# Cross attention of a gated decoder by whole sequences, with stacked hi/lo scores and a sum by a product, on one Trainium2 core

## The chip, the core and the metric

The kernel runs on one core of one Trainium2 chip. The metric is the device time of one execution in microseconds. The engines of a core are TensorE (PE; its weight loads are listed as PEld), VectorE (DVE), ScalarE (ACT), GpSimd (POOL) and SyncE (SP), each with its own queue of instructions, taken in the order in which they were written; they wait for one another through semaphores. SyncE's and ScalarE's queues also issue DMA transfers. Products go from SBUF to PSUM, which has 8 banks of 512 float32 columns.

## The reference

There are 16 sequences of 256 queries with 128 features, and 64 context rows for each. Cross attention has 16 heads of 8 features. What the change touches is this, once per layer:

```python
q, k, v = heads(norm(x) @ Wq.T [+ bq]), heads(ctx @ Wk.T [+ bk]), heads(ctx @ Wv.T [+ bv])
scores = einsum('bhqd,bhkd->bhqk', q, k) / sqrt(8)
scores = where(causal, scores, -inf)      # layer 0 only: key <= query
scores = where(mask, scores, -inf)        # layer 1: -1e10
out = softmax(scores) @ v
x = x + tanh(g) * (merge(out) @ Wo.T [+ bo])
```

Between the two cross attentions come two layers of local attention with an MLP, and at the end a mixture of experts; these are not changed.

## The kernel before

The program is a row of stages with all engines meeting between them: `Setup`, `Cross` for layer 0, `Local` and `Mlp` twice, `Cross` for layer 1, `Experts`. Setup loads the constants, computes keys (`kT`, features by keys) and values (`vall`) of all sequences and the rows of the masks.

`Cross` goes by tiles of 128 queries, 32 in all, two per sequence. `tensor`, `scalar`, `vector` and `gpsimd` each hold a loop over steps `s`, in which several tiles are at different points: in step `s` tile `s-2` is transposed, `s-3` becomes q, `s-4` gets its scores, `s-5` is transposed back, and so on up to `s-9`. The order within a step is written out by hand and is the order of that engine's queue. `after` waits for a count that frees a buffer.

For a tile, VectorE takes statistics (L225, L227), GpSimd the root (L232, L234), VectorE normalizes (L238), TensorE transposes (L412), ScalarE copies (L484), TensorE forms q (L419). ScalarE rounds q to the reduced-precision float32r as `qT` (L490), VectorE keeps the rest `qTr` (L550 in layer 0, L547 in layer 1). Keys are split in the same way into `kTh` (L513) and `kTr` (L515), and for each sequence GpSimd spreads both into block form, 128 features by 16 heads x 64 keys (L594). Scores are three products for each half of 512 columns (L438 to L440), a causal part from a 64-row identity (L442, only layer 0 and even tiles) and the pad row (L444, one row). VectorE takes the negated maxima (L564) and adds them (L567) into SBUF, ScalarE takes the exponential (L478). TensorE transposes that in eight parts (L458), ScalarE copies it (L503), and L468 multiplies it with `vpair`, in which each pair of heads has 32 columns: values, and two columns of ones, so that sums of the exponentials come out beside the values. ScalarE copies (L509), TensorE transposes (L425), VectorE takes the reciprocal of the sums (L529) and multiplies (L531), TensorE transposes once more (L451), ScalarE copies (L497), L403 is the output projection, L405 the bias of layer 1 from one row, and L520 updates x. In layer 0, the stage also normalizes the updated x into y (L225 to L238), which local attention reads.

SyncE issues only loads of later weights: 21 transfers in layer 0 (L185 to L205) and three of expert weights in layer 1 (L210 to L212).

## Time and profile before

| | us |
|---|---|
| three runs, median (lowest to highest) | 1428.67 (1428.21 to 1429.47) |
| profiled execution, its own time | 1427.41 |
| its span in the profile | 1425.6 |
| TensorE busy | 1276.2 (90%) |
| VectorE busy | 1107.3 (78%) |
| ScalarE busy | 832.5 (58%) |
| GpSimd busy | 866.1 (61%) |

A row of a view of busy times gives a stretch in us from the span's start, its length, then for PE, PEld, DVE, ACT and POOL the busy time and the number of instructions, then the granted clock of TensorE as a share of 2.4 GHz, the DMA engines' share and GB/s. A row of the timeline gives start, duration, engine, line, operation, output and inputs, shapes, how many were merged, and in brackets the idle time before it with what ended it. A row of a group gives line, engine, operation, names, shapes, count, then busy us and the mean in ns, then the idle time before it. Matmuls are pipelined: the distance of two starts is what one costs, its duration holds a latency. An f32 product that is not a transpose is two instructions.

### The profile page before, as it was taken

Reading aid. Unit: us, or ns where it says so; the run is one execution under the profiler, and the core shown is the slowest. Engines: PE = TensorE matmul, PEld = TensorE weight load, DVE = VectorE, ACT = ScalarE, POOL = GpSimd, SP = SyncE. Lnnn points to the kernel's source line nnn. Section 1 sums busy time; section 2 is a strip of 40 time slices with the busy share of each in tenths; the row PEclk is TensorE's granted clock in tenths of the full one; section 3 lists DMA queues with packets and bytes.
Section 4 is the critical chain, followed back from the end, with each engine's and each line's share of the span. In section 5 each row is a group of like instructions: output and inputs, shape, how many; then the busy total and the mean of one; then the engine's idle time right before and its main releaser. Section 6 shows DMA issues by size and latency. Waiting matters only on the chain.

```text
span 1425.6 us, 32359 instructions
## 1 busy us (share of the span) xinstructions
PE 1276.2 (90%) x10920; PEld 1053.8 (74%) x10920; DVE 1107.3 (78%) x2582; ACT 832.5 (58%) x2379; POOL 866.1 (61%) x1006
## 2 busy tenths in 40 slices
PE   4999995799999985966999999969879999899998
PEld 2566563688888875965888888859846666699997
DVE  5588886899999963857999999738857777488887
ACT  1355553577777762535777777735435555466664
POOL 1566662999999962328999999823255544143332
PEclk8799997899999997988999999979979999899999
DMA  7000000000000001110000000001110000000000
GB/s 198 7 2 1 1 1 13 9 9 9 10 9 10 2 2 51 34 31 14 9 10 10 9 9 4 2 15 31 32 30 1 1 2 1 1 13 13 15 12 14
DMA packets 57460, 23.12 MB, mean 16 GB/s; under 512 B 46629, under 2 KB 55122, under 8 KB 57298
## 3 DMA queue, kind: packets, MB, share of 16 engines
q1 hardware_dynamic: 55120, 19.22, 5.5%
q10 hardware_dynamic: 2178, 1.83, 0.5%
q8 instruction: 91, 1.49, 0.4%
q14 instruction: 71, 0.58, 0.1%
HBM read 10.56 MB, written 2.10 MB: 9 GB/s over the span
## 4 chain that ended last, share of the span: by engine, by line
PE 77%; DVE 6%; issue 6%; ACT 4%; POOL 4%; DMA 1%; SPq 1%; DVEq 0%; ACTq 0%; POOLq 0%
PE a_ps_s L711 6%; PE m_ps_h L1133 6%; PE m_ps_y L1143 6%; PE a_ps_b L745 4%; PE x_ps_t L458 4%; PE a_ps_t L755 4%; PE a_ps_t L729 4%; PE a_ps_a L774 4%; PE x_ps_s L438 3%; PE f_ps_y L1006 3%; PE f_ps_g L1015 3%; PE f_ps_a L1020 3%; PE x_ps_s L444 3%; ACT a_e L807 2%; PE x_ps_s L440 2%
## 5 line engine op out<-in xcount | busy, mean ns | idle before, releaser
L941 POOL TENSOR_TENSOR a_stat<-a_stat,small 128x16 f32<-128x16 f32 x64 | 186.9, 2921 | 5.3
L807 ACT ACTIVATE a_e<-a_ps_s,a_stat 128x128 f32<-128x128 f32 x512 | 179.6, 378 | 3.0 <-DVE a_stat L870 2.1
L711 PEld LDWEIGHTS a_ps_s<-a_kTr,a_qbd 128*128 128x128 f32 x1024 | 134.9, 192 | 4.1
L951 POOL TENSOR_TENSOR a_e<-a_e,a_stat 128x1024 f32<-128x1024 f32 x64 | 121.4, 1897 | 22.5 <-DVE a_stat L901 22.5
L711 PE MATMUL a_ps_s<-a_kTr,a_qbd 128*128 128x128 f32 x1024 | 134.9, 275 | 0.0
L945 POOL TENSOR_TENSOR a_rot<-a_rot,a_stat 128x1024 f32<-128x1024 f32 x64 | 121.8, 1904 | 5.0
L564 DVE TENSOR_REDUCE x_stat<-x_ps_s 128x16 f32<-128x1024 f32 x64 | 78.0, 1219 | 54.0 <-PE x_ps_s L444 54.0
L807 ACT ACTIVATION_READ_ACCUMULATOR a_e<-a_ps_s,a_stat 128x1 f32 x512 | 111.4, 218 | 0.0
L232 POOL TENSOR_SCALAR x_st<-x_st 128x1 f32<-128x1 f32 x96 | 21.3, 222 | 146.5 <-DVE x_st L227 137.9
L914 DVE TENSOR_TENSOR a_rot<-a_ps_qk,a_rtab 128x512 f32<-128x512 f32 x128 | 87.7, 685 | 26.5 <-ACT a_sq L814 26.3
L937 POOL TENSOR_TENSOR a_rot<-a_rot 128x512 f32<-128x512 f32 x64 | 82.5, 1289 | 39.4 <-DVE a_rot L917 38.8
L800 ACT ACTIVATE a_eT<-a_ps_t 128x1024 f32<-128x1024 f32 x64 | 65.5, 1023 | 60.2 <-PE a_ps_t L729 60.2
L503 ACT ACTIVATE x_eT<-x_ps_t 128x1024 f32<-128x1024 f32 x64 | 65.5, 1024 | 54.9 <-PE x_ps_t L458 54.9
L1133 PE MATMUL m_ps_h<-m_hT,w 128*128 128x128 f32 x768 | 95.5, 282 | 0.0
L917 DVE TENSOR_TENSOR a_rot<-a_ps_qk,a_rtab 128x256 f32<-128x256 f32 x256 | 95.3, 413 | 0.0
L896 DVE COPY a_qbd<-a_ps_t 64x512 f32<-64x512 f32 x128 | 87.8, 686 | 6.9 <-PE a_ps_t L755 4.9
L1143 PE MATMUL m_ps_y<-w,m_up 128*128 128x128 f32 x768 | 91.1, 275 | 1.5 <-DVE m_yw L1180 1.5
L1133 PEld LDWEIGHTS m_ps_h<-m_hT,w 128*128 128x128 f32 x768 | 90.3, 195 | 0.0
L1042 ACT ACTIVATE f_gl<-f_ps_g,vec 128x128 f32<-128x128 f32 (+1 forms) x192 | 55.8, 361 | 58.5 <-PE f_ps_g L1015 58.4
L1143 PEld LDWEIGHTS m_ps_y<-w,m_up 128*128 128x128 f32 x768 | 88.3, 192 | 1.6 <-issue 1.6
L755 PE MATMUL a_ps_t<-c,a_rot 128*128 128x128 f32 x512 | 69.9, 281 | 19.1 <-POOL a_rot L945 9.6
L870 DVE TENSOR_REDUCE a_stat<-a_ps_s 128x8 f32<-128x1024 f32 x64 | 77.6, 1212 | 9.8 <-PE a_ps_s L711 9.8
(169 smaller groups left out, 3751.8 us busy)
## 6 DMA issues: line engine op xcount, KB each, us to landing
a_h<-y SPq DMA_DIRECT2D x64, 32.0 KB
f_h<-y SPq DMA_DIRECT2D x64, 32.0 KB
out_dram<-x SPq DMA_DIRECT2D x32, 64.0 KB, 1.5
a_h<-y SPq DMA_DIRECT2D x64, 31.8 KB
f_h<-y SPq DMA_DIRECT2D x64, 31.8 KB
wqkv<-in_L_ffn_wqkv_dram SPq DMA_DIRECT2D x2, 768.0 KB, 4.3
w<-in_L_ffn_w_dram SPq DMA_DIRECT2D x2, 768.0 KB, 5.5
c_ctx2T<-in_ctxT_dram SPq DMA_DIRECT2D x2, 512.0 KB, 3.3
```

Of the source, the lines that this page charges most:

```text
L711: m = pe.matmul(ps_s[:, at:at + P].rearrange("p (w k) -> p w k", k=WIN), self.qbd[u][:, at:at + P], ky, start=False, stop=(c == 3))
L755: m = pe.transpose(ps_t[:, P * i:P * i + P], self.rot[n % 2][:, P * i:P * i + P], g.ident)
L807: act.activation(self.e[n % 2][:, P * i:P * i + P], self.ps_s[:, P * i:P * i + P], ACT.Exp, bias=stat[:, i:i + 1], accum_out=stat[:, 8 + i ...
L896: v.tensor_copy(dst, ps_t[LD * e:LD * e + LD, 0:512].rearrange("p (r q) -> p r q", q=WIN)).then_inc(self.s_qc, 1)
L914: v.tensor_tensor(out1, qk, cos_.unsqueeze(1).broadcast_to([P, LH, LD]), ALU.mult).then_inc(self.s_r, 1)
L917: v.tensor_tensor(out2[:, :, lo:lo + LD // 2], qk[:, :, hi:hi + LD // 2], sin_[:, lo:lo + LD // 2].unsqueeze(1).broadcast_to([P, LH, LD // ...
L937: p.tensor_tensor(r, r, self.rot2[:, INNER:], ALU.add).then_inc(self.s_n, 1)
L941: p.tensor_tensor(t[:, 48:64], t[:, 32:48], g.neg_half.broadcast_to([P, 16]), ALU.pow).then_inc(self.s_n, 1)
L945: p.tensor_tensor(r, r, t[:, 48:64].unsqueeze(2).broadcast_to([P, 16, LD]), ALU.mult).then_inc(self.s_n, 1)
L951: p.tensor_tensor(e3, e3, self.stat[n % 2][:, 16:24].unsqueeze(2).broadcast_to([P, 8, P]), ALU.mult)\
L1133: m = pe.matmul(self.ps_h[b][:, P * i:P * i + P], g.w1[:, P * c:P * c + P], self.hT[n % 2][:, :], start=True, stop=True)
L1143: m = pe.matmul(self.ps_y[:, D * e:D * e + D], self.up[n % 2][:, P * c:P * c + P], g.w2[:, D * c:D * c + D], start=(i == 0), stop=(i == w ...
```

## The change

`Cross` now goes by sequences (16 per layer) instead of tiles. A step `s` still holds several sequences at different points, in an order written out by hand.

- Four heads are stacked along the contraction. The hi and lo parts of q (both 256 queries wide) are stored by SyncE to DRAM and loaded back in three transfers into `stack`: rows 0 to 31 hi, 32 to 63 hi again, 64 to 95 lo, for four groups of four heads side by side; row 96 is one. `kblk` has the matching rows of keys (hi, rest, hi) and the pad row; GpSimd fills it from `ksrc` with one operation for a sequence. `ksrc` is filled at the stage's begin by 16 transfers, and four more put one-hot rows into rows 97 to 112 of the four `kblk`. A score product is now one of 97 rows over 256 columns.
- First scores (queries by keys) serve for the maxima only. The negated maxima are transposed (16 by 256), copied and brought into rows 97 to 112 of `stack` by a transfer. Second scores of 113 rows are computed by key (keys on the partitions, queries along the columns), with the maxima subtracted inside the product, so the exponentials, taken straight from PSUM, need no transpose.
- Values by `vblk`, and the sums by a product with a constant `osel`, give outputs and sums by feature over 256 queries. VectorE takes the reciprocal of 128x256 sums and multiplies; the result is the stationary operand of the projection, with no further transpose.
- The causal part stays a bf16 product with 64 rows: in the first scores over 256 columns for each of four groups of tile 0, in the second scores over 64 columns for each of the eight products.
- y in layer 0 is written by ScalarE, with mean and root from GpSimd. Statistics and updates go two tiles at a time.
- The mask of layer 0 is no longer multiplied into the values; two transfers of 4 KB and two small VectorE operations fall away in the setup. `padrow` becomes float32. In the stages before and after, nothing else changes.

The core of the diff, cut to the new orders of SyncE, TensorE and VectorE:

```diff
+    n_src = 16 * (4 * 4 + RING)
+    def sync_begin(self, sp, l):
+        sp.wait_ge(self.s_kh, l + 1)
+        sp.wait_ge(self.s_kr, l + 1)
+        for j in range(XG):
+            at, rows = slice(B * SC * j, B * SC * j + B * SC), slice(32 * j, 32 * j + 32)
+            sp.dma_start(self.ksrc[0:32, at], self.kTh[rows, :].bitcast(F32)).then_inc(self.s_src, 16)
+            sp.dma_start(self.ksrc[32:64, at], self.kTr[rows, :]).then_inc(self.s_src, 16)
+            sp.dma_start(self.ksrc[64:96, at], self.kTh[rows, :].bitcast(F32)).then_inc(self.s_src, 16)
+            sp.dma_start(self.ksrc[96:97, at], self.g.padrow[l][:, :]).then_inc(self.s_src, 16)
+        sp.wait_ge(self.s_oh, l + 1)
+        for t in self.kblk:
+            sp.dma_start(t[97:97 + XH, :].bitcast(F32), self.oneh[:, :].bitcast(F32)).then_inc(self.s_src, 16)
+    def sync(self, sp, l, s):
+        b = s - 2
+        if 0 <= b < B:
+            k = B * l + b
+            r, rows = k % RING, self.g.xq[k % RING]
+            after(sp, self.s_t, 2 * (k - RING + 1))
+            sp.wait_ge(self.s_qs[r], 16 * (k // RING + 1))
+            for i in range(3):
+                src = rows[:, S * (i // 2):S * (i // 2) + S].rearrange("(j r) c -> r j c", j=XG)
+                dst = self.stack[r][32 * i:32 * i + 32, :].rearrange("r (j c) -> r j c", j=XG)
+                sp.dma_start(dst.bitcast(F32), src).then_inc(self.s_qd[r], 16)
+        b = s - 1
+        if 0 <= b < B:
+            k = B * l + b
+            r = k % RING
+            after(sp, self.s_qd[r], 48 * (k // RING))
+            sp.wait_ge(self.s_qh, k + 1)
+            sp.wait_ge(self.s_ql, k + 1)
+            sp.dma_start(self.g.xq[r], self.q[b % 2][:, :].bitcast(F32)).then_inc(self.s_qs[r], 16)
+        b = s - 3
+        if 0 <= b < B:
+            k = B * l + b
+            sp.wait_ge(self.s_mc, k + 1)
+            dst = self.stack[k % RING][97:97 + XH, :].rearrange("r (j c) -> r j c", j=XG)
+            src = self.mT[b % 2][0:XH, :].unsqueeze(1).broadcast_to([XH, XG, S])
+            sp.dma_start(dst.bitcast(F32), src.bitcast(F32)).then_inc(self.s_md[k % RING], 16)
+    def scores(self, pe, l, b, t):
+        k = B * l + b
+        if t == 0:
+            pe.wait_ge(self.s_qd[k % RING], 48 * (k // RING + 1))
+            pe.wait_ge(self.s_kb, k + 1)
+        after(pe, self.s_mx, 2 * k + t)
+        for j in range(XG):
+            at = slice(S * j, S * j + S)
+            m = pe.matmul(self.ps_s[:, at], self.stack[k % RING][0:97, S * j + P * t:S * j + P * t + P], self.kblk[k % RING][0:97, at],
+                          start=True, stop=bool(l or t))
+            if not l and t == 0:
+                m = pe.matmul(self.ps_s[:, at], self.g.ident16[0:SC, :], self.g.causal[:, 0:SC].unsqueeze(1).broadcast_to([SC, 4, SC]),
+                              start=False, stop=True)
+        m.then_inc(self.s_s, 1)
+    def shifted_scores(self, pe, l, b, half):
+        k = B * l + b
+        if half == 0:
+            pe.wait_ge(self.s_md[k % RING], 16 * (k // RING + 1))
+        after(pe, self.s_e, 2 * k + half)
+        for i in range(4):
+            j, dst = 2 * half + i // 2, self.ps_t[:, S * i:S * i + S]
+            at = S * j + P * (i % 2)
+            m = pe.matmul(dst, self.kblk[k % RING][0:113, at:at + P], self.stack[k % RING][0:113, S * j:S * j + S], start=True, stop=bool(l))
+            if not l:
+                m = pe.matmul(dst[:, 0:SC], self.g.causal, self.g.ident16[0:SC, 0:SC], start=False, stop=True)
+        m.then_inc(self.s_t, 1)
...
+    def tensor_begin(self, pe, l):
+        pe.wait_ge(self.s_src, self.n_src * (l + 1))
+        pe.wait_ge(self.s_z, (RING + 2) * (l + 1))
+    def tensor(self, pe, l, s):
+        g = self.g
+        b = s - 3
+        if 0 <= b < B:
+            self.scores(pe, l, b, 0)
+        b = s - 1
+        if 0 <= b < B:
+            k = B * l + b
+            pe.wait_ge(self.s_nm, 2 * k + 2)
+            after(pe, self.s_xc, k)
+            after(pe, self.s_mc, k - 2)
+            for t in range(2):
+                m = pe.transpose(self.ps_x[:, P * t:P * t + P], self.h[b % 2][:, P * t:P * t + P], g.ident)
+            m.then_inc(self.s_x, 1)
+        b = s - 5
+        if 0 <= b < B:
+            self.shifted_scores(pe, l, b, 0)
+        b = s - 1
+        if 0 <= b < B:
+            k = B * l + b
+            pe.wait_ge(self.s_xc, k + 1)
+            after(pe, self.s_qh, k)
+            after(pe, self.s_ql, k)
+            pe.matmul(self.ps_q[:, 0:S], g.wq[l][:, :], self.hT[b % 2][:, :], start=True, stop=True).then_inc(self.s_q, 1)
+        b = s - 6
+        if 0 <= b < B:
+            k = B * l + b
+            pe.wait_ge(self.s_on, 2 * k + 2)
+            after(pe, self.s_up, k)
+            for t in range(2):
+                dst = self.ps_w[:, D * t:D * t + D]
+                m = pe.matmul(dst, self.on[b % 2][:, P * t:P * t + P], g.wo[l][:, :], start=True, stop=not l)
                 if l:
+                    m = pe.matmul(dst, g.ones_row[:, :], g.bfc[:, :], start=False, stop=True)
+            m.then_inc(self.s_w, 1)
+        b = s - 3
+        if 0 <= b < B:
+            self.scores(pe, l, b, 1)
+        b = s - 5
+        if 0 <= b < B:
+            k = B * l + b
+            self.shifted_scores(pe, l, b, 1)
+            pe.wait_ge(self.s_vb, 2 * k + 2)
+            pe.wait_ge(self.s_e, 2 * k + 2)
+            after(pe, self.s_on, 2 * k)
+            for i in range(2):
+                e = [self.eT[2 * (b % 2) + j // 2][:, 512 * (j % 2) + S * i:512 * (j % 2) + S * i + S] for j in range(XG)]
+                for j in range(XG):
+                    at = 64 * j + 32 * i
+                    pe.matmul(self.ps_o[32 * j:32 * j + 32, 0:S], self.vblk[b % 2][:, at:at + 32], e[j], start=(i == 0), stop=(i == 1))
+            for i in range(2):
+                e = [self.eT[2 * (b % 2) + j // 2][:, 512 * (j % 2) + S * i:512 * (j % 2) + S * i + S] for j in range(XG)]
+                for j in range(XG):
+                    m = pe.matmul(self.ps_o[32 * j:32 * j + 32, S:2 * S], g.osel[:, 32 * i:32 * i + 32], e[j], start=(i == 0),
+                                  stop=(i == 1))
+            m.then_inc(self.s_o, 1)
+        b = s - 3
+        if 0 <= b < B:
+            k = B * l + b
+            pe.wait_ge(self.s_mx, 2 * k + 2)
+            pe.wait_ge(self.s_xc, min(k + 3, B * l + B))
+            after(pe, self.s_mc, k)
+            for t in range(2):
+                m = pe.transpose(self.ps_x[0:XH, S + P * t:S + P * t + P], self.mx[b % 2][:, XH * t:XH * t + XH], g.ident)
+            m.then_inc(self.s_m, 1)
...
+    def maxima(self, v, l, b, t):
+        k = B * l + b
+        v.wait_ge(self.s_s, 2 * k + t + 1)
+        if t == 0:
+            after(v, self.s_m, k - 1)
+        v.tensor_reduce(self.mx[b % 2][:, XH * t:XH * t + XH], self.ps_s[:, :].rearrange("p (h k) -> p h k", k=SC), AX_X, ALU.max,
+                        negate=True).then_inc(self.s_mx, 1)
+    def vector(self, v, l, s):
         g = self.g
+        b = s - 1
+        if 0 <= b < B:
+            k, st = B * l + b, self.st[b % 2]
+            v.wait_ge(self.s_rs, 2 * k + 2)
+            after(v, self.s_x, k - 1)
+            for t in range(2):
+                v.tensor_scalar(self.h[b % 2][:, P * t:P * t + P], tok(g.x, 2 * b + t), st[:, 12 + 2 * t:13 + 2 * t],
+                                st[:, 18 + t:19 + t], ALU.subtract, ALU.mult).then_inc(self.s_nm, 1)
+        b = s - 3
+        if 0 <= b < B:
+            self.maxima(v, l, b, 0)
+        b = s - 6
+        if 0 <= b < B:
+            k = B * l + b
+            v.wait_ge(self.s_o, k + 1)
+            after(v, self.s_w, k - 1)
+            v.reciprocal(self.inv[b % 2][:, :], self.ps_o[:, S:2 * S]).then_inc(self.s_on, 1)
+            v.wait_ge(self.s_on, 2 * k + 1)
+            v.tensor_tensor(self.on[b % 2][:, :], self.ps_o[:, 0:S], self.inv[b % 2][:, :], ALU.mult).then_inc(self.s_on, 1)
+        b = s - 1
+        if 0 <= b < B:
+            k = B * l + b
+            v.wait_ge(self.s_qh, k + 1)
+            i = (k - 2) % RING
+            after(v, self.s_qs[i], 16 * ((k - 2) // RING + 1) if k > 1 else 0)
+            if l:
+                v.scalar_tensor_tensor(out=self.q[b % 2][:, S:2 * S], in0=self.ps_q[:, 0:S], scalar=g.bq, in1=self.q[b % 2][:, 0:S],
+                                       op0=ALU.add, op1=ALU.subtract).then_inc(self.s_ql, 1)
+            else:
+                v.tensor_tensor(self.q[b % 2][:, S:2 * S], self.ps_q[:, 0:S], self.q[b % 2][:, 0:S], ALU.subtract).then_inc(self.s_ql, 1)
+        b = s
+        if 0 <= b < B:
+            k = B * l + b
+            after(v, self.s_nm, 2 * (k - 1))
+            self.statistics(v, self.s_st, k, self.st[b % 2], g.x[:, S * b:S * b + S])
+        b = s - 6
+        if 0 <= b < B:
+            k = B * l + b
+            v.wait_ge(self.s_w, k + 1)
+            v.scalar_tensor_tensor(out=g.x[:, S * b:S * b + S], in0=self.ps_w[:, 0:S], scalar=g.tg[:, l:l + 1],
+                                   in1=g.x[:, S * b:S * b + S], op0=ALU.mult, op1=ALU.add).then_inc(self.s_up, 1)
+        b = s - 3
+        if 0 <= b < B:
+            self.maxima(v, l, b, 1)
+        b = s - 6
+        if not l and 0 <= b < B:
+            v.wait_ge(self.s_up, b + 1)
+            after(v, self.s_yn, 2 * (b - 1))
+            self.statistics(v, self.s_yst, b, self.yst[b % 2], g.x[:, S * b:S * b + S])
```

ScalarE's step: the copy of h transposed (`s-1`), exponentials of half 0 (`s-5`), q's hi part (`s-1`), exponentials of half 1 (`s-5`), y (`s-7`, layer 0), the copy of the transposed maxima (`s-3`). GpSimd's step: the root of the statistics of sequence `s`; in layer 0 the root, the negated mean and their product for y of `s-7`; the `kblk` of `s-2` (one tensor_tensor over 97x1024); the two copies into `vblk` of `s-4`. Before its loop it waits, as TensorE does, for all of `s_src`.

## Rows read from the trace of the kernel before

**Rows 1.** Busy times of one stretch in each cross stage (columns: see above)

```profile
120.00:126.00 6.00, 5.94 (x43) 3.65 (x44) 4.74 (x13) 3.20 (x7) 3.57 (x6) 1.00 0.00 0
...
1122.00:1128.00 6.00, 6.00 (x46) 3.89 (x46) 4.36 (x10) 3.06 (x6) 5.06 (x7) 1.00 0.01 3
```

**Rows 2.** Timeline: the same weight load one sequence apart, per layer

```profile
119.87 0.19 PEld L438 LDWEIGHTS x_ps_s<-x_kblk,x_qT 128*128 128x128 f32 x1 [0.23 <-issue]
...
131.14 0.19 PEld L438 LDWEIGHTS x_ps_s<-x_kblk,x_qT 128*128 128x128 f32 x1 [0.23 <-issue]
...
1119.88 0.19 PEld L438 LDWEIGHTS x_ps_s<-x_kblk,x_qT 128*128 128x128 f32 x1
...
1130.81 0.19 PEld L438 LDWEIGHTS x_ps_s<-x_kblk,x_qT 128*128 128x128 f32 x1
```

**Rows 3.** Timeline: first transpose and last write of each cross stage

```profile
31.74 0.18 PEld L412 LDWEIGHTS x_ps<-c,x_h 128*128 128x128 f32 x1 [10.56 <-issue]
...
234.62 0.35 DVE L238 TENSOR_SCALAR y<-x,x_st 128x128 f32<-128x128 f32 x1 [0.98 <-POOL x_st L234]
...
1035.71 0.18 PEld L412 LDWEIGHTS x_ps<-c,x_h 128*128 128x128 f32 x1 [6.38 <-issue]
...
1229.46 0.35 DVE L520 SCALAR_TENSOR_TENSOR x<-x_ps,small,x 128x128 f32<-128x128 f32 x1 [2.52 <-PE x_ps L405]
```

**Rows 4.** Timeline, layer 0: products of 1, 128 and 64 rows in turn

```profile
121.09 0.39 PE L444 MATMUL x_ps_s<-padrow,c 1*128 1x512 bf16 x1
...
121.40 0.50 PE L438 MATMUL x_ps_s<-x_kblk,x_qT 128*128 128x512 f32 x1
...
121.74 0.39 PE L439 MATMUL x_ps_s<-x_kblkr,x_qT 128*128 128x512 f32 x1
...
121.97 0.40 PE L440 MATMUL x_ps_s<-x_kblk,x_qTr 128*128 128x512 f32 x1
...
122.30 0.39 PE L442 MATMUL x_ps_s<-c 64*128 64x512 bf16 x1
```

**Rows 5.** Groups by line and shape, VectorE: product, reduction, two reciprocals

```profile
L917 DVE TENSOR_TENSOR a_rot<-a_ps_qk,a_rtab 128x256 f32<-128x256 f32 x256 | 95.3, 413 | 0.0
...
L564 DVE TENSOR_REDUCE x_stat<-x_ps_s 128x16 f32<-128x1024 f32 x64 | 78.0, 1219 | 54.0 <-PE x_ps_s L444 54.0
...
L529 DVE RECIPROCAL x_stat<-x_ps 128x16 f32<-128x16 f32 x64 | 16.4, 256 | 15.2 <-PE x_ps L425 14.9
...
L901 DVE RECIPROCAL a_stat<-a_stat 128x8 f32<-128x8 f32 x64 | 13.0, 203 | 20.3 <-ACT a_e L807 17.1
```

**Rows 6.** Timeline: value products; projection in layer 1 and what follows

```profile
124.06 0.64 PE L468 MATMUL x_ps<-x_eT,x_vpair 128*32 128x128 f32 x16
...
1124.01 0.49 PE L403 MATMUL x_ps<-wo,x_onT 128*128 128x128 f32 x2
...
1124.84 0.33 PE L412 MATMUL x_ps<-c,x_h 128*128 128x128 f32 x1
```

**Rows 7.** Groups by line and shape, ScalarE: copy of 1024 columns from PSUM

```profile
L503 ACT ACTIVATE x_eT<-x_ps_t 128x1024 f32<-128x1024 f32 x64 | 65.5, 1024 | 54.9 <-PE x_ps_t L458 54.9
```

**Rows 8.** Timeline: first and last of SyncE's 21 transfers; kTr of layer 1

```profile
27.50 0.33 SPq L185 DMA_DIRECT2D wqkv<-in_L_ffn_wqkv_dram  x1
...
36.92 0.28 SPq L205 DMA_DIRECT2D mw<-in_L_ffn_b_dram  x1
...
1031.76 1.22 DVE L515 TENSOR_TENSOR x_kTr<-kT,x_kTh 128x1024 f32<-128x1024 f32 x1
```

**Rows 9.** DMA issues: KB each and us to landing of the output's stores

```profile
out_dram<-x SPq DMA_DIRECT2D x32, 64.0 KB, 1.5
```

**Rows 10.** Busy times and granted clock of four stretches

```profile
48.00:54.00 6.00, 5.87 (x18) 3.43 (x17) 3.37 (x6) 2.30 (x4) 1.55 (x3) 0.50 0.00 0
...
222.00:228.00 6.00, 4.48 (x52) 2.93 (x51) 3.11 (x13) 2.23 (x5) 1.56 (x4) 1.00 0.00 0
...
228.00:234.00 6.00, 1.54 (x5) 0.74 (x4) 3.19 (x13) 0.28 (x1) 2.56 (x7) 0.51 0.01 1
...
264.00:272.00 8.00, 4.59 (x36) 3.87 (x35) 6.74 (x13) 6.78 (x23) 7.79 (x6) 1.00 0.04 9
```

More of the change, by code:

```diff
@@ L22 @@
 XH, XD = 16, 8
-XP = XH // 2
+XG = XH // 4
+RING = 4
 LH, LD, WIN = 8, 64, 64
@@ L80, in constants @@
     causal = np.where(k[None, :] > p[:, None], AWAY, 0).astype(f)
-    c16 = np.concatenate([np.eye(P, dtype=f), np.ones((P, P), f), causal, m.reshape(P, -1)], 1)
+    c16 = np.concatenate([np.eye(P, dtype=f), causal, causal, m.reshape(P, -1)], 1)
     return np.ascontiguousarray(c32), np.ascontiguousarray(c16.astype(f))
@@ L366, in begin @@
+        self.s_qd = first.s_qd if first else [g.sem(f"x_qd{i}") for i in range(RING)]
+        self.s_qs = first.s_qs if first else [g.sem(f"x_qs{i}") for i in range(RING)]
+        self.s_md = first.s_md if first else [g.sem(f"x_md{i}") for i in range(RING)]
     def begin(self, l):
         self.room(l)
-        self.st, self.st2, self.stat = self.many("st", 2, 16), self.many("st2", 2, 16), self.many("stat", 2, 2 * XH)
-        self.h, self.hT = self.many("h", 2, D), self.many("hT", 2, D)
-        self.qT, self.qTr = self.many("qT", 2, D, F32R), self.many("qTr", 2, D, F32R)
+        self.ksrc = self.sb("ksrc", XG * B * SC)
@@ L381, in totals @@
     def totals(self, l):
-        k, pairs = T * (l + 1), T // 2
-        done = [(self.s_z, 6 if l else 2), (self.s_kb, 2 * pairs * (l + 1)), (self.s_kh, l + 1), (self.s_kr, l + 1),
-                (self.s_vb, 3 * pairs + 2 * pairs * l), (self.s_sm, 2 * k), (self.s_on, 2 * k)]
-        done += [(s, k) for s in (self.s_h, self.s_hc, self.s_q, self.s_qc, self.s_qr, self.s_s, self.s_e, self.s_t,
-                                  self.s_tc, self.s_o, self.s_oc, self.s_w, self.s_up, self.s_ot, self.s_nt, self.s_nc)]
@@ new lines, in totals @@
+        done += [(s, 48 * ((k - 1 - i) // RING + 1)) for i, s in enumerate(self.s_qd)]
+        done += [(s, 16 * ((k - 1 - i) // RING + 1)) for i, s in enumerate(self.s_qs)]
+        return done + [(s, 16 * ((k - 1 - i) // RING + 1)) for i, s in enumerate(self.s_md)]
+    n_src = 16 * (4 * 4 + RING)
[11 more added lines that the diff above has]
+            sp.dma_start(t[97:97 + XH, :].bitcast(F32), self.oneh[:, :].bitcast(F32)).then_inc(self.s_src, 16)
@@ L1253, in _ @@
             settle(sp, setup.totals())
-            cross[0].sync(sp, 0)
+            load_attention_weights(sp, g, 0)
+            load_mlp_weights(sp, g, 0)
+            cross[0].sync_begin(sp, 0)
+            for s in range(Cross.STEPS):
+                cross[0].sync(sp, 0, s)
             settle(sp, cross[0].totals(0))
@@ L1265, in _ @@
             settle(sp, mlp[1].totals(1))
-            cross[1].sync(sp, 1)
+            load_expert_weights(sp, g)
+            cross[1].sync_begin(sp, 1)
+            for s in range(Cross.STEPS):
+                cross[1].sync(sp, 1, s)
             settle(sp, cross[1].totals(1))
@@ L1273, in _ @@
             settle(pe, setup.totals())
-            cross[0].tensor(pe, 0)
+            cross[0].tensor_begin(pe, 0)
+            for s in range(Cross.STEPS):
+                cross[0].tensor(pe, 0, s)
             settle(pe, cross[0].totals(0))
@@ L1283, in _ @@
             settle(pe, mlp[1].totals(1))
-            cross[1].tensor(pe, 1)
+            cross[1].tensor_begin(pe, 1)
+            for s in range(Cross.STEPS):
+                cross[1].tensor(pe, 1, s)
             settle(pe, cross[1].totals(1))
@@ L1291, in _ @@
             settle(act, setup.totals())
-            cross[0].scalar(act, 0)
+            cross[0].scalar_begin(act, 0)
+            for s in range(Cross.STEPS):
+                cross[0].scalar(act, 0, s)
             settle(act, cross[0].totals(0))
@@ L1301, in _ @@
             settle(act, mlp[1].totals(1))
-            cross[1].scalar(act, 1)
+            cross[1].scalar_begin(act, 1)
+            for s in range(Cross.STEPS):
+                cross[1].scalar(act, 1, s)
             settle(act, cross[1].totals(1))
@@ L1309, in _ @@
             settle(v, setup.totals())
-            cross[0].vector(v, 0)
+            cross[0].vector_begin(v, 0)
+            for s in range(Cross.STEPS):
+                cross[0].vector(v, 0, s)
             settle(v, cross[0].totals(0))
@@ L1319, in _ @@
             settle(v, mlp[1].totals(1))
-            cross[1].vector(v, 1)
+            cross[1].vector_begin(v, 1)
+            for s in range(Cross.STEPS):
+                cross[1].vector(v, 1, s)
             settle(v, cross[1].totals(1))
@@ L1327, in _ @@
             settle(p, setup.totals())
-            cross[0].gpsimd(p, 0)
+            cross[0].gpsimd_begin(p, 0)
+            for s in range(Cross.STEPS):
+                cross[0].gpsimd(p, 0, s)
             settle(p, cross[0].totals(0))
@@ L1337, in _ @@
             settle(p, mlp[1].totals(1))
-            cross[1].gpsimd(p, 1)
+            cross[1].gpsimd_begin(p, 1)
+            for s in range(Cross.STEPS):
+                cross[1].gpsimd(p, 1, s)
             settle(p, cross[1].totals(1))
```

405 lines of the change are left out of this document (150 added, 255 removed).

## The prediction

> **What bounds the kernel now.** I read first the busy times of two six-microsecond stretches, one in each cross-attention stage: TensorE is busy for 5.94 and 6.00 of 6.00 us at a granted clock of 1.00, VectorE for 4.74 and 4.36 [rows 1]. So TensorE's queue sets the pace. Then the same weight load two tiles apart, which is one sequence: 11.27 us in layer 0 and 10.93 us in layer 1 [rows 2]. Then the stages' edges: from the first transpose of h to the last write, 31.74 to 234.97 (203.2 us) and 1035.71 to 1229.81 (194.1 us) [rows 3]. The change must be judged against these four numbers. The rest of the program is untouched; in the setup two 4 KB transfers and two short VectorE operations go, behind which nothing waited, and I cost that at nothing.
>
> **What the change removes.** Per sequence (256 queries) TensorE loses 12 score products over 512 columns plus 4 of the pad row, 2 causal ones, 16 transposes of e and 6 of od and on. VectorE loses two passes over 1024 columns, ScalarE two copies. If throughput counted alone, this would be a large gain. But every engine takes its work in a fixed order, so I follow the chain of one step.
>
> **The chain of a full step.** TensorE's order is: first scores (tile 0), transposes of h, shifted scores (half 0), q, output projection of the sequence three steps back, first scores (tile 1), shifted scores (half 1), value and sum products, transposes of the maxima. VectorE takes the maxima of tile 0 ahead of the reciprocal and the product that the projection waits for. So one step is a closed ring, and its parts are (layer 0 / layer 1):
> - First scores, tile 0. A product over 512 columns starts 0.23 us after the one before it (121.74 to 121.97); where a product over 128 rows follows or is followed by one over 64 rows or 1 row it is 0.34, 0.33 and 0.31 [rows 4]. 512 columns stream in 0.21 at full clock, so a change of rows costs some 0.13 behind, 0.12 ahead of a 128-row product and 0.10 behind the short one. 97 and 113 rows I take as 128. With 256 columns each, a pair of a score product and a causal one (64 rows) is 0.11+0.25+0.11+0.10 = 0.56. Four pairs to the start of the reduction, with 0.22 of latency: 3x0.56+0.36+0.11+0.22 = **2.37**. Layer 1 has no causal part: 0.13+3x0.11+0.28+0.05 = **0.79**.
> - Maxima 1.22 [rows 5]. The reciprocal over 128x256 is shown nowhere. Below, it costs what another operation of 256 columns costs, 0.41; above, 16 of the 128x16 ones, 4.1. The rows say that it is slow per element: 8 elements 203 ns, 16 elements 256 ns, so 6.6 ns each, 256+240x6.6 = **1.8**. I take this because it is a slope of the same operation. The product that follows is 0.41 [rows 5], with 0.08 between engines. Together **3.5**. Meanwhile TensorE has h, half 0 and q, 2.7 us (layer 1: 1.3), all hidden; without that cover they would lengthen the step by as much.
> - Projection: two products at 0.22 each and a change of columns 0.1, **0.55**; in layer 1 projection and bias are 0.83 per tile, 124.01 to 124.84 [rows 6], **1.66**. First scores, tile 1: 4x0.11 = **0.45**.
> - Shifted scores, half 1: a pair with a causal part of 64 columns is 0.36+0.03+0.10 = 0.49, so 3x0.49+0.36+0.25 = **2.08**; layer 1 **0.66**. Exponentials over 1024 columns from PSUM, as the copy, 1.02 [rows 7], plus 0.05: **1.07**. TensorE has nothing else between, so this is a stall.
> - Values and sums: before, 16 instructions of 128 columns in 32-column tiles, 16x0.107/4 = 0.43, which the row bears out (0.64 with 0.27 of latency) [rows 6]. Now four times the columns: 1.71 plus 0.1, **1.81**. Maxima's transposes with their two changes of width: **0.42**.
> Sums: 2.37+3.5+0.55+0.45+2.08+1.07+1.81+0.42 = **12.25** against 11.27, and 0.79+3.5+1.66+0.45+0.66+1.07+1.81+0.42 = **10.36** against 10.93. The columns that were saved come back as waits in a ring.
>
> Rule against row: what the row bears is 6.6 ns an element. The Trainium skill, VectorE: DVE Perf Modes, section First, the fixed hardware budget, says that the reciprocal repeats its divide step eight times. At the 0.96 GHz that the page gives this would be 8.3 ns, an estimate of 2.1 us for the reciprocal and some 10 us more over the kernel. I go by the row.
>
> **The start of each stage.** TensorE and GpSimd now wait for 20 more transfers (16 for ksrc, 4 for kblk) before anything. SyncE issued 21 transfers from 27.50 to 37.20, 0.46 each [rows 8]. In layer 0 the 20 stand behind those: issued at 37.2+9.2 = 46.4, landed 1.5 to 2 later (out_dram lands in 1.5 [rows 9]), 48.3. Statistics' root and norm 1.6: first transpose at 49.9 instead of 31.74, **+18.2**. In layer 1 they begin once kTr is done, 1032.98 [rows 8]: 1042.2, 1044.0, first transpose 1045.5 instead of 1035.71, **+9.8**.
>
> **Filling and draining.** At stage begin the clock was 0.50 [rows 10], so columns cost double. First transpose to q's two parts 3.0, store 2.1, loads 3.0: 8.1. Then two steps with only scores and maxima (layer 0: 3.2+1.22+1.2+1.22+0.6 = 7.4; layer 1: 5.4), and one in which shifted scores, exponentials and products come in at double price (15.6 and 10.7): 38.6 and 29.6 to the first full step. 13 full steps: 159.3 and 134.7. Two without first scores: 15.8 and 15.2. Last: 6.5 (with y) and 4.6. Stage from first transpose: 220.2 against 203.2, **+17.0**; 184.1 against 194.1, **-10.0**. With the starts: +35.2 and -0.2, together +35.0.
> The profiled execution took 1427.4 (span 1425.6), 1.3 under the median of 1428.7, within 0.2%, about the least that a measurement of this kernel tells from nothing. Clock held: 1427.4+35 = 1462.
>
> **The clock.** Each ring now has two idle stretches of TensorE (in layer 1 2.2 us under VectorE and 1.1 under the exponentials), and columns stream for under half of the step. The rows go both ways: a stretch with TensorE busy 4.48 of 6 kept 1.00 and fell to 0.5 at once behind it; one with 4.59 of 8 kept 1.00 throughout [rows 10]. On the ring 4.2 and 4.1 us are streaming, which double at 1.2 GHz. I take a third of the steps' work at 1.2 GHz, 1.4 us x 26 full steps and 1 us x 4: +40. **Forecast: 1502.**
>
> Costs set to nothing: SyncE's five transfers a step (5x0.47 = 2.4 us of 10 to 12); a sequence's store has the rest of its step, its loads the next whole step, so 6 us and more of cover; if that failed, first scores would wait 2 to 3 us a step. SyncE's load stands ahead of its store and its wait for the maxima behind both: harmless while a step is over 6 us. GpSimd has one 1.9 us block where it had two, ScalarE some 3.5 us of work.
>
> **Rivals.**
> - The clock holds at 1.00 in the full steps: 1462. For it the last of rows 10, against it the second and third. The Trainium skill, TensorE: Matmul & The Clock Gate, section Why this matters for your kernels, says that a throughput drop inside a kernel comes from idle gaps longer than the ones worked out here; by that rule it is this rival. 28%.
> - The clock is 0.5 nearly throughout, since each step's idle stretches return: 1462+4.2x26+3x4 = 1583. 12%.
> - Faster: the reciprocal takes the 0.41 of an ordinary operation. It stands 32 times on the ring: 1462-32x1.4 = 1417. It decides below 1.8-35/32 = 0.7 us, with the clock held. The slope in rows 5 speaks against it. 8%.
> - The transfers through DRAM bound the step, or the sixteen ksrc copies land much later than a store does: 2 us x 32, 1526 or more. 4%.
> The forecast itself has 48%, from 1480 to 1525.
>
> **Range and chances.** 1425 takes in short changes of rows (0.05 instead of 0.12 gives -1 us a step) and a partly cheaper reciprocal; 1560 a clock that is low for more than half of the time and the page's reciprocal. Left out: most of the faster case and the upper end of the slow one. Slower 0.90, same 0.02, faster 0.08.
>
> **What the new profile would show.** A RECIPROCAL of 128x256 near 1.8 us, ahead of each projection; step periods (start to start of first scores) of 12.2 or more and 10.4 or more; first transposes near 50 and 1045; PEclk tenths of 6 to 9 in both stages instead of 9; TensorE idle behind ACT's exponential once a step. I am wrong if the reciprocal is under 0.7 us, if changes of rows cost nothing with 97 rows, or if the stages are shorter than 203 and 194 us.

## The result, and the profile after

The changed kernel takes **1591.92 us** (median of 4, 1590.05 to 1595.64), against 1428.99 for the kernel before in the same runs: 1.1144 times as long, 95% interval 1.1121 to 1.1167. The forecast was 1502, in a range of 1425 to 1560. The direction was right; of the 163 us that it lost I had forecast 73.

The page of the changed kernel, with the granted clock in 40 slices:

```profile
span 1588.6 us, 30533 instructions
PE 1304.9 (82%) x10376; PEld 1064.3 (67%) x10376; DVE 1047.0 (66%) x2356; ACT 752.6 (47%) x2187; POOL 793.5 (50%) x902
PEclk8556556559999999797999999979756666689999
```

Busy times and granted clock of the changed kernel: its two cross-attention stages, from the first transpose to the last write, and a fast and a slow stretch of the first:

```profile
55.60:332.20 276.60, 227.45 (x1120) 131.25 (x1120) 120.63 (x250) 62.66 (x112) 74.06 (x142) 0.59 0.14 42
1151.20:1392.90 241.70, 171.56 (x992) 110.30 (x992) 112.22 (x186) 52.40 (x81) 52.32 (x78) 0.66 0.16 48
151.00:158.00 7.00, 6.15 (x41) 3.45 (x33) 3.75 (x5) 2.06 (x4) 0.00 (x0) 0.97 0.23 66
159.00:181.00 22.00, 19.68 (x95) 11.33 (x98) 9.36 (x23) 5.74 (x10) 9.07 (x17) 0.50 0.13 43
```

The stages take 276.6 and 241.7 us, where the kernel before takes 203.2 and 194.1 [rows 3]. The mean clock in them is 0.59 and 0.66. TensorE is "busy" for 82% of the first stage, nearly as in the slow stretch (19.68 of 22) and the fast one (6.15 of 7): busy time doesn't tell the two clock levels apart, since a product at 1.2 GHz is busy for longer and a change of rows counts as busy (183.20 below starts 0.50 behind 182.70 with no idle time between).

One step of layer 0 in TensorE's timeline. The clock falls on its way (between 188.3 and 189.6):

```profile
182.70 0.36 PE L450 MATMUL x_ps_s<-x_kblk,x_stack 97*128 97x256 f32 x1
182.99 0.28 PE L453 MATMUL x_ps_s<-c 64*128 64x256 bf16 x1
183.20 0.38 PE L450 MATMUL x_ps_s<-x_kblk,x_stack 97*128 97x256 f32 x1
...
188.29 0.71 PE L506 MATMUL x_ps<-wo,x_on 128*128 128x128 f32 x4 [0.85 <-DVE x_on L627]
188.76 1.03 PE L450 MATMUL x_ps_s<-x_kblk,x_stack 97*128 97x256 f32 x4
...
193.35 1.94 PE L524 MATMUL x_ps<-x_eT,x_vblk 128*32 128x256 f32 x16 [1.16 <-issue]
195.02 1.97 PE L528 MATMUL x_ps<-x_eT,c 128*32 128x256 f32 x16
196.92 0.60 PE L538 MATMUL x_ps<-c,x_mx 128*16 128x128 f32 x2
197.17 0.56 PE L450 MATMUL x_ps_s<-x_kblk,x_stack 97*128 97x256 f32 x1
```

And VectorE's in the same step:

```profile
184.89 1.22 DVE L604 TENSOR_REDUCE x_mx<-x_ps_s 128x16 f32<-128x1024 f32 x1 [6.60 <-PE x_ps_s L453]
186.03 1.75 DVE L625 RECIPROCAL x_inv<-x_ps 128x256 f32<-128x256 f32 x1
187.81 0.42 DVE L627 TENSOR_TENSOR x_on<-x_ps,x_inv 128x256 f32<-128x256 f32 x1
```

This is the ring as forecast. The first scores of tile 0 take 182.70 to 184.89, 2.19 (forecast 2.37; a pair is 0.50 to 0.53 from start to start, forecast 0.56). Maxima, reciprocal and product take until 188.23 (3.34, forecast 3.5), and TensorE idles 0.85 ahead of the projection. Behind the second exponentials it idles 1.16 (1.07). The value and sum products take 3.57 here, at half clock, against 1.81 forecast at full clock. The reciprocal takes 1747 to 1758 ns in its 32 cases, forecast 1.8: the slope held. The estimate of 2.1 us by the Trainium skill, VectorE: DVE Perf Modes, section First, the fixed hardware budget, does not agree with these rows.

In layer 1 the longest idle time lies ahead of the projection too. It is 2.05 or less, but for the last two full steps (2.96 and 2.97):

```profile
1194.77 0.49 PE L506 MATMUL x_ps<-wo,x_on 128*128 128x128 f32 x2 [2.05 <-DVE x_on L627]
...
1343.02 0.80 PE L506 MATMUL x_ps<-wo,x_on 128*128 128x128 f32 x2 [2.96 <-DVE x_on L627]
```

### The profile page after: what moved, and what is told of

Read it like the earlier page. It is cut to its first block and busy times, and to the rows that moved or that the text cites. A ratio compares the mean times of both kernels' runs of the same rounds, so it can differ in the third digit from the quotient of the medians.

```text
span 1588.6 us, 30533 instructions
## 1 busy us (share of the span) xinstructions
PE 1304.9 (82%) x10376; PEld 1064.3 (67%) x10376; DVE 1047.0 (66%) x2356; ACT 752.6 (47%) x2187; POOL 793.5 (50%) x902
## 3 DMA queue, kind: packets, MB, share of 16 engines
q10 hardware_dynamic: 2018, 1.81, 0.4%
## 5 line engine op out<-in xcount | busy, mean ns | idle before, releaser
L604 DVE TENSOR_REDUCE x_mx<-x_ps_s 128x16 f32<-128x1024 f32 x64 | 78.1, 1221 | 176.8 <-PE x_ps_s L453 104.7
L672 POOL TENSOR_SCALAR x_st<-x_st 128x2 f32<-128x2 f32 x32 | 7.0, 220 | 283.6 <-DVE x_st L592 253.1
L570 ACT ACTIVATE x_eT<-x_ps_t 128x1024 f32<-128x1024 f32 x32 | 32.7, 1023 | 141.5 <-PE x_ps_t L466 81.3
L450 PE MATMUL x_ps_s<-x_kblk,x_stack 97*128 97x256 f32 x256 | 84.0, 436 | 16.5 <-issue 11.7
L466 PE MATMUL x_ps_t<-x_stack,x_kblk 113*128 113x256 f32 x256 | 93.7, 433 | 0.3 <-ACT x_eT L557 0.2
L524 PE MATMUL x_ps<-x_eT,x_vblk 128*32 128x256 f32 x512 | 61.0, 624 | 37.2 <-issue 33.6
```

The source lines that it names most:

```text
L450: m = pe.matmul(self.ps_s[:, at], self.stack[k % RING][0:97, S * j + P * t:S * j + P * t + P], self.kblk[k % RING][0:97, at], start=True, ...
L466: m = pe.matmul(dst, self.kblk[k % RING][0:113, at:at + P], self.stack[k % RING][0:113, S * j:S * j + S], start=True, stop=bool(l))
```

## The experiments

All times below are compared with the kernel before on the same chip (its medians were 1429.0 to 1430.0). "Full step" is the mean of eleven distances from one sequence's reciprocal (in e8 its copy) to the next one's, the second to the twelfth of these distances, in layer 0 / layer 1. An edit is shown against the changed kernel.

| kernel | us | ratio to before (95%) | full step | mean clock |
|---|---|---|---|---|
| changed | 1591.9 | 1.114 (1.112 to 1.117) | 15.2 / 13.6 | 0.83 |
| e1_fill | 1506.7 | 1.054 (1.051 to 1.057) | 13.1 / 10.3 | 0.91 |
| e2_fill2 | 1543.6 | 1.080 (1.077 to 1.084) | 13.9 / 11.6 | 0.92 |
| e3_rows | 1544.1 | 1.080 (1.077 to 1.083) | 12.0 / 13.8 | 0.86 |
| e4_recfirst | 1502.4 | 1.052 (1.048 to 1.055) | 12.4 / 9.4 | 0.89 |
| e5_start | 1564.7 | 1.096 (1.093 to 1.099) | 15.1 / 13.7 | 0.84 |
| e6_order | 1519.8 | 1.065 (1.062 to 1.068) | 13.7 / 10.4 | 0.86 |
| e7_kblk | 1584.2 | 1.108 (1.106 to 1.110) | 15.1 / 13.7 | 0.84 |
| e8_copy | 1514.9 | 1.063 (1.057 to 1.069) | 12.6 / 10.6 | 0.88 |
| c7_steps (e3, e4, e6) | 1424.4 | 0.997 (0.994 to 0.999) | 9.9 / 8.1 | 0.90 |
| c8_all (c7, e5) | 1399.4 | 0.977 (0.972 to 0.982) | 9.9 / 8.1 | 0.91 |
| c9_all2 (c8, e7) | 1370.3 | 0.959 (0.957 to 0.961) | 7.8 / 8.3 | 0.92 |
| c10_all3 (c9, products) | 1361.0 | 0.952 (0.950 to 0.954) | 7.8 / 8.1 | 0.93 |

**Idle products: is it the clock?**

```
+    def filler(self, pe, dst, n):
+        for i in range(n):
+            pe.matmul(dst[:, :], self.g.ident16, self.g.c16[:, 0:512], start=True, stop=True)
...
+            after(pe, self.s_up, k)
+            self.filler(pe, self.ps_w, (4, 10)[l])
             pe.wait_ge(self.s_on, 2 * k + 2)
...
+            self.filler(pe, self.ps_o, (4, 4)[l])
             pe.wait_ge(self.s_vb, 2 * k + 2)
```

> The changed kernel with idle products put into TensorE's two stalls of each step (ident16 times 512 columns of c16, into banks that TensorE owns just then): 4 in layer 0 and 10 in layer 1 ahead of the projection's wait, 4 ahead of the wait for the second exponentials. Their results are overwritten. At full clock they take 0.85, 2.1 and 0.85 us and fit into the stalls. Clock theory (the rings are as forecast, 12.3 and 10.4 us, and what the forecast missed is TensorE at 1.2 GHz for most of both stages): with the stalls filled the clock stays up in the full steps, the periods go from 15.4 and 13.5 to about 12.4 and 10.6, 26 steps, so some 75 us less: 1515. Rival (the steps are long for another reason, transfers or engine waits, and the clock is only a companion): the periods stay or grow by what the products take at 1.2 GHz beyond the stalls, some 1.4 us a step: 1590 to 1630.

> As the run with idle products, but 8 (layer 0) and 14 (layer 1) ahead of the projection and 8 ahead of the value products, so that they no longer fit: 1.7 us a step over. Clock theory: the clock is held with certainty, periods 14.1 and 12.3, total about 1515+26x1.7 = 1560, still under 1592 although TensorE does more. Rival: 26 x 2.8 to 3.4 us on top of 1592, 1665 or more.

Both totals came out as the clock theory has it, and e2 is the stronger of the two: with 8, 14 and 8 products, more than the stalls hold, it is still 48 us faster than the kernel that lacks them (1543.6 against 1591.9). What the theory called certain held in layer 1 alone: in layer 0 of e2 the clock still fell at times, and its steps go from 12.7 to 15.9. Waits for transfers or engines would not shrink when work is added to the engine on the ring. Stretches of e1_fill that lie within its two stages:

```profile
55.60:300.00 244.40, 214.86 (x1248) 122.03 (x1248) 128.59 (x256) 64.48 (x113) 76.53 (x146) 0.79 0.16 48
1115.00:1310.00 195.00, 167.26 (x1214) 105.45 (x1214) 113.81 (x187) 52.47 (x81) 52.88 (x78) 0.91 0.20 60
```

A step of its layer 1 in TensorE's timeline, from first scores to first scores of the next sequence (10.32 us):

```profile
1225.80 0.72 PE L450 MATMUL x_ps_s<-x_kblk,x_stack 97*128 97x256 f32 x4
...
1228.02 2.32 PE L477 MATMUL x_ps<-c 128*128 128x512 bf16 x10
1230.18 0.38 PE L511 MATMUL x_ps<-wo,x_on 128*128 128x128 f32 x2
...
1236.12 0.72 PE L450 MATMUL x_ps_s<-x_kblk,x_stack 97*128 97x256 f32 x4
```

The clock is 0.79 and 0.91 there, after 0.59 and 0.66. In layer 1 the full steps are 10.2 to 10.3 without exception; the forecast's ring at held clock is 10.36. In layer 0 the fast steps are 11.53 (forecast 12.25), but others still take 12.9 to 17.0: there the products didn't suffice.

**Changes of rows.**

```
-        self.causal = c16[0:WIN, P:2 * P]
+        self.causal = c16[:, P:2 * P]
...
-                m = pe.matmul(self.ps_s[:, at], self.g.ident16[0:SC, :], ...
+                m = pe.matmul(self.ps_s[:, at], self.g.ident16, ...
...
-                m = pe.matmul(dst[:, 0:SC], self.g.causal, self.g.ident16[0:SC, 0:SC], start=False, stop=True)
+                m = pe.matmul(dst[:, 0:SC], self.g.causal, self.g.ident16[:, 0:SC], start=False, stop=True)
```

> The changed kernel with the causal products of layer 0 over all 128 rows (the constants have zeros there; the sum is the same) instead of 64. Theory (each change between a 97- or 113-row product and a 64-row one costs 0.10 to 0.13 us, 16 changes a step on the ring): a pair of a score and a causal product takes 0.22 instead of 0.53 at full clock, a shifted pair 0.14 instead of 0.45, the ring of layer 0 shrinks by 2.1 us or more, 16 sequences, 34 to 50 us less, 1545 to 1558; layer 1 unchanged. Rival (the cost belongs to the change of type or of tile width, not of rows): no change, 1592.

48 us less (1544.1, just under the expected 1545 to 1558), all in layer 0. TensorE's timeline of e3_rows, two pairs of the first scores of tile 0 at full clock:

```profile
159.58 0.36 PE L450 MATMUL x_ps_s<-x_kblk,x_stack 97*128 97x256 f32 x1
159.79 0.28 PE L453 MATMUL x_ps_s<-c 128*128 128x256 bf16 x1
159.83 0.36 PE L450 MATMUL x_ps_s<-x_kblk,x_stack 97*128 97x256 f32 x1
160.04 0.28 PE L453 MATMUL x_ps_s<-c 128*128 128x256 bf16 x1
```

A pair costs 0.25 instead of 0.50 to 0.53, with twice the rows, the same columns and the same types. So the price lies in going from 97 rows to 64 and back, not in the type; 97 and 128 rows mix almost freely, as the prediction took them (0.25 for a pair, where it had 0.21 for 512 columns). The edit also bears on the clock: the mean clock of the full steps of layer 0 rises from 0.62 to 0.78, although TensorE is now idle for 25% of that time instead of 11%. Whether it is the change between products that counts or the rows themselves (128 for 64), no run separates. In these rows of busy times, the changed kernel comes first and then e3_rows:

```profile
125.00:290.00 165.00, 146.38 (x758) 85.78 (x757) 73.49 (x162) 41.65 (x74) 51.46 (x101) 0.62 0.15 45
...
114.00:246.00 132.00, 98.56 (x766) 65.40 (x765) 73.88 (x164) 42.27 (x75) 51.57 (x101) 0.78 0.20 59
```

**The reciprocal.** In e4 the seven lines of reciprocal and product stand ahead of the two of `self.maxima(v, l, b, 0)` in VectorE's step; in e8 `v.reciprocal(...)` is `v.tensor_copy(...)`.

> The changed kernel with VectorE's reciprocal and product of a sequence ahead of the maxima of tile 0 in the step, instead of behind. Theory (1.75 us reciprocal is on the ring only because it stands behind the maxima): its operand is ready when the step begins, so it now runs under the maxima's transposes and the first scores; TensorE no longer idles ahead of the projection (0.85 us in layer 0, 1.3 to 2.2 in layer 1): 10 to 15 us less in layer 0, 17 to 30 in layer 1, some more if the clock rises with it: 1535 to 1565. Rival (VectorE is late with the maxima instead, and the second tile's first scores wait for as long): no change within 5 us.

> The changed kernel with a copy in place of the reciprocal (left out: the division by the sums; the product multiplies by them). It asks what the change would give if the reciprocal took the time of an ordinary operation of 256 columns, 0.41 us instead of 1.75. By the ring: 1.34 us a step less wherever TensorE idles ahead of the projection for that long, 0.85 in layer 0, 1.34 in layer 1, 30 to 40 us over the kernel, and 10 to 40 more from the clock: 1510 to 1555. The faster case of the prediction (1417 with a cheap reciprocal) presumed a held clock: it would need 1430 or less here.

e4 gave 90 us (1502.4), more than expected (1535 to 1565). A step of its layer 1 in TensorE's timeline:

```profile
1165.52 0.72 PE L450 MATMUL x_ps_s<-x_kblk,x_stack 97*128 97x256 f32 x4
...
1167.20 0.70 PE L498 MATMUL x_ps<-x_hT,wq 128*128 128x256 f32 x2
1167.78 0.49 PE L506 MATMUL x_ps<-wo,x_on 128*128 128x128 f32 x2
...
1173.83 0.72 PE L450 MATMUL x_ps_s<-x_kblk,x_stack 97*128 97x256 f32 x4
```

The projection now follows q with no idle time, and the step is 8.3 us at full clock. The step at held clock is shorter by 2.0 (10.3 to 8.3); that the mean fell by 4.2 (13.6 to 9.4) is the clock, which such steps keep in part. e8, which takes 1.33 us off the same place (416 ns for 1749), gave 77 us: a reciprocal at an ordinary price would have left the change at 1515, not at the 1417 of the prediction's faster case. The clock would still fall (its mean is 0.88), and the starts and fills that the prediction had too short stay.

**The start.**

```
-            load_attention_weights(sp, g, 0)
-            load_mlp_weights(sp, g, 0)
             cross[0].sync_begin(sp, 0)
...
+                if s == B + 2:
+                    load_attention_weights(sp, g, 0)
+                    load_mlp_weights(sp, g, 0)
...
     def scalar_begin(self, act, l):
-        pass
+        self.sync_begin(act, l, 1)
```

(`sync_begin` takes half of the four heads' groups; the waits for `s_src` go to the first scores and the first kblk.)

> The changed kernel with another start of both stages: the 20 ksrc and kblk transfers are issued half by SyncE and half by ScalarE, ahead of layer 0's weight loads (which go to step 19), and TensorE and GpSimd wait for them only at the first scores and the first kblk. The full steps are untouched. Theory (the transfers cost 0.63 us of SyncE each, and all wait for them): first transposes 17 us earlier in layer 0 and 12 in layer 1, first scores by 12 to 18 and 8 to 12: 1562 to 1572. Rival (the transfers are bound by the DMA engines, two queues share them): only the weight loads' 9.7 us in layer 0 are won, 1580.

1564.7, within what was expected. The start in SyncE's and TensorE's timelines of the changed kernel:

```profile
39.06 0.64 SPq L405 DMA_DIRECT2D x_ksrc<-x_kTh  x1
...
49.25 2.48 SPq L411 DMA_DIRECT2D x_kblk<-x_oneh  x4
...
55.63 0.66 PE L487 MATMUL x_ps<-c,x_h 128*128 128x128 f32 x2 [32.04 <-DVE x_h L615]
```

In e5 TensorE's first transpose and first scores of layer 0:

```profile
36.92 0.66 PE L488 MATMUL x_ps<-c,x_h 128*128 128x128 f32 x2 [13.74 <-DVE x_h L616]
...
50.64 0.55 PE L452 MATMUL x_ps_s<-x_kblk,x_stack 97*128 97x256 f32 x1 [4.77 <-POOL x_kblk L708]
```

The first scores are 18 us earlier (68.59 to 50.64). Two queues issue side by side, each at its 0.6 us a transfer: the issuing engine was the limit, not the transfer.

**The order of the shifted scores.**

```
+        b = s - 5
+        if 0 <= b < B:
+            self.shifted_scores(pe, l, b, 1)
         b = s - 6
         if 0 <= b < B:
             k = B * l + b
             pe.wait_ge(self.s_on, 2 * k + 2)
...
-            self.shifted_scores(pe, l, b, 1)
```

> The changed kernel with TensorE's shifted scores of half 1 directly behind q, ahead of the projection and the first scores of tile 1. Theory (the second exponentials, 1.07 us, stand on the ring because nothing lies between the shifted scores and the value products): projection and scores of tile 1 (1.0 us, layer 1 2.1) now run under them, and half 1 itself under VectorE's reciprocal: 1.0 us a step less in layer 0 and 1.7 in layer 1, 35 us, and more where the clock rises: 1530 to 1557. Rival (half 1 now waits for the first exponentials, in front of the projection, for as long as it saves): 1585 to 1600.

72 us less (1519.8), twice what the ring alone gives (35) and more than expected (1530 to 1557). The rest goes with the clock, whose mean rises from 0.83 to 0.86; no run separates the two. Layer 0 shows something more. The clock still falls in every step there, although TensorE has hardly any idle time left: in this stretch of e6_order, which is two steps, it is busy for the whole 28.00 us at a mean clock of 0.62.

```profile
157.00:185.00 28.00, 28.00 (x144) 15.81 (x140) 14.43 (x32) 8.13 (x14) 9.34 (x18) 0.62 0.18 52
```

So the idle stretches are not the whole cause in layer 0. What e3 changed, the rows of the causal products, has a part in it.

**The fill.** In e7 the block of GpSimd's `kblk` stands at the head of the step, ahead of `self.root(p, self.s_rs, ...)`.

> The changed kernel with GpSimd's kblk of a sequence at the head of its step, ahead of the root that waits for the statistics of that step, instead of behind. Theory (in the fill a step is 10.4 us because it is a ring too: first scores 3.3, transposes and q 2.4, its two parts 0.8, statistics 1.1, root 0.9, kblk 1.9, and the first scores of the next): kblk leaves that ring, so the fill's four or five steps of each stage are 1.9 us shorter, 10 to 18 us less; the full steps of 15.2 and 13.6 are bound elsewhere and stay: 1574 to 1582. Rival (the fill waits for the stack's loads, 5 us from the store's issue to their landing): 1588 to 1595.

7.7 us less (1584.2), a little under the expected. Rows of the changed kernel's timelines (GpSimd, VectorE, TensorE) in the fill of layer 0:

```profile
75.93 0.22 POOL L672 TENSOR_SCALAR x_st<-x_st 128x2 f32<-128x2 f32 x1 [7.48 <-DVE x_st L592]
76.23 0.71 POOL L674 TENSOR_TENSOR x_st<-x_st,small 128x2 f32<-128x2 f32 x1
77.02 1.89 POOL L706 TENSOR_TENSOR x_kblk<-x_ksrc,c 97x1024 fp32r<-97x1024 f32 x1
...
76.98 2.27 DVE L615 TENSOR_SCALAR x_h<-x,x_st 128x128 f32<-128x128 f32 x2
...
79.02 0.55 PE L450 MATMUL x_ps_s<-x_kblk,x_stack 97*128 97x256 f32 x1 [1.42 <-issue]
```

First scores start 0.11 behind kblk's end, kblk behind the root, the root behind statistics that stand behind q's second part, and q behind the first scores of the step before: the fill is a ring of its own, 10.42 us long (79.02 to 89.44). In e7 TensorE's first scores of two such steps are 8.66 apart:

```profile
76.77 0.56 PE L450 MATMUL x_ps_s<-x_kblk,x_stack 97*128 97x256 f32 x1
...
85.43 0.56 PE L450 MATMUL x_ps_s<-x_kblk,x_stack 97*128 97x256 f32 x1
```

**Together.**

> The three edits to the step together: causal products over 128 rows, reciprocal ahead of the maxima, shifted scores of half 1 ahead of the projection. By the ring's terms the full steps go to 8.0 to 9.5 us in layer 0 and 8.0 to 9.0 in layer 1 (from 15.2 and 13.6), 130 to 150 us less: 1440 to 1465, with the start and the fill as they are. Rival (another engine bounds the step then, VectorE at 7.5 us of work with its waits, or SyncE's chain of store and loads): steps of 10 us and more, 1480 or above.

> The three edits to the step and the other start. If the parts add up: c7_steps less the 20 to 30 us of e5_start, 1410 to 1445, that is, about the kernel before or under it.

> All edits so far: the three to the step, the other start, kblk at the head of the step. In the run before it (without the last edit) the first scores of layer 0 began 0.1 us behind kblk's end, TensorE idle for 1.66 us once a step of 9.7 us, and the fill's steps waited likewise. If kblk was the last thing that bound it: layer 0 at 8.0 to 8.6, 14 to 22 us less there, 5 to 10 in the fills: 1365 to 1382. If VectorE's norm, which took 2.2 us instead of 0.83 beside kblk, bounds it next: 1385 to 1399.

> The run with all edits and 3 idle products of 512 columns ahead of the shifted scores of half 1, where TensorE waits 0.6 to 1.1 us for the first exponentials. If the clock still falls in the steps and costs more than the products take: 5 to 15 us less than without them. If the steps are short enough to keep it: the same, or up to 10 us more.

The three edits to the step give 167 us together (1424.4, where 1440 to 1465 was expected; one by one they gave 48, 90 and 72): the change with its ring mended is level with the kernel before (0.997). With the other start it is 1399.4, under the expected 1410 too. That is 2.3% faster than the kernel before, with an interval of 1.8% to 2.9%, although layer 0 hung on kblk there, in GpSimd's and TensorE's timelines of c8_all:

```profile
136.49 1.89 POOL L710 TENSOR_TENSOR x_kblk<-x_ksrc,c 97x1024 fp32r<-97x1024 f32 x1 [0.17 <-POOL x_yst L697]
...
138.48 0.36 PE L452 MATMUL x_ps_s<-x_kblk,x_stack 97*128 97x256 f32 x1 [1.66 <-issue]
```

With kblk earlier the full step of layer 0 goes from 9.9 to 7.8; layer 1's grows from 8.1 to 8.3. Both totals came out as expected, c9's and c10's. The clock is 1.00 in c9's full steps of layer 0, although TensorE still waits for the first exponentials once a step (0.60 us):

```profile
90.00:165.00 75.00, 66.81 (x657) 49.72 (x655) 66.42 (x142) 36.82 (x67) 45.14 (x89) 1.00 0.31 94
...
125.11 0.39 PE L468 MATMUL x_ps_t<-x_stack,x_kblk 113*128 113x256 f32 x1 [0.60 <-ACT x_eT L560]
```

c10 is 9 us under c9, with the same full steps in layer 0. Its 96 idle products win mainly in the last steps of each stage (6 us), where c9's periods still rise to 8.8 and 9.2 and c10's stay at 7.6 and below, and some 2 us in the full steps of layer 1, where the clock goes from 0.94 to 1.00. This is the fastest version, 1361.0 us, 4.8% under the kernel before.

## Why the prediction was wrong in size

- **The clock, forecast +40: the step that failed.** I took a third of the steps' work at 1.2 GHz, 1.4 us a full step. Measured means are 15.19 and 13.60; the same rings at full clock are 11.54 and 10.31 (e1). So the clock costs 3.65 and 3.29 a full step, 90 us over 26, not 36. The rival "0.5 nearly throughout" had 4.2 and 1583, which is nearest to the result; the longest full steps, 15.79 and 14.25, are indeed 4.25 and 3.94 over the ring. I gave it 12%, because single stretches of [rows 10] with less busy time had kept the clock. But the one that kept it throughout (4.59 of 8) stood between dense stretches of the kernel before:

```profile
256.00:264.00 8.00, 8.00 (x43) 6.71 (x43) 7.31 (x13) 3.63 (x12) 7.84 (x5) 0.82 0.03 7
...
272.00:280.00 8.00, 7.18 (x74) 6.12 (x73) 6.83 (x14) 5.72 (x21) 7.75 (x6) 1.00 0.05 10
```

Here the stalls return in every step. My third was a mean between "held" and "lost" with no row behind it; measured is 87% and 80% of the whole loss.
- **The rival "clock holds", 28%,** fell, and with it the rule behind it. The Trainium skill, TensorE: Matmul & The Clock Gate, section Why this matters for your kernels, gives longer idle gaps than these as what to avoid against throughput drops inside a kernel. The trace doesn't agree that this is enough: idle times ahead of a product in the full steps of the changed kernel are 0.85 and 1.16 in layer 0, and up to 2.05 in layer 1 with 2.96 and 2.97 at its end, and the clock was at 0.59 and 0.66 over the stages. Filling the stalls raised it (e1), so short gaps that return do it too; and in layer 0 of e6 it fell without a gap, so they aren't all of it. What the rest is, and how much each counts, stays open; e3 shows that the 64-row products have a part in it.
- **The ring, 12.25 and 10.36:** right; 11.54 and 10.31. Layer 0 is 0.7 shorter, over 13 steps 9 us in the other direction. In a fast step of e1 (129.54 to 141.08) the second shifted scores take 1.79 (forecast 2.08) and the maxima's transposes 0.14 (0.42); every other term is within 0.2. The pair of the first scores, written as 0.56, adds up to 0.57 from its own terms, which changes nothing.
- **The starts, +18.2 and +9.8:** measured first transposes at 55.63 against 49.9, and 19.9 behind the stage's begin in layer 1 where before it was 5.3, so +14.6. A ksrc transfer costs SyncE 0.63, not the 0.46 that I took from the weight loads; 20 of them make 3.4 us, and the rest is landing, GpSimd's release, and in layer 0 some 2 us by which the setup ended later in this execution. Together 10 us too few.
- **The fill, 38.6 and 29.6:** measured 49.6 and 39.4 (first transpose to the first full step), 21 us too few. I had costed kblk at nothing, as one 1.9 us block of GpSimd with cover in the full steps. In the fill it has none: it closes a second ring of 10.4 us in layer 0, where I had 7.4. Taking kblk off it gave 7.7 us (e7); the rest of the 21 no run takes apart.
- **Draining:** 29.5 and 25.5 behind the full steps, 5 and 4 us above the forecast. It goes with the clock: in e1 the last three distances of layer 0 are together 8.6 us shorter.
- **SyncE's five transfers and the stack through DRAM** cost nothing in the full steps, as said: TensorE has no idle time ahead of a score product there, but for 0.69 us in the first of layer 1, where kblk ended 0.11 before it. The rival of 4% fell.

The sum: 20 and 24 in the full steps, 21 in the fills, 10 in the starts, 9 in the draining, 84 of the 88 by which the profiled execution (1590.4) missed 1502; the rest is spread over the stages that were not changed.
